# Four stacked-score attention phases: transposes three units back, the values of a sequence in one block, the first queries stacked from two queues

## The chip, the cores and the metric

The kernel runs on one core of a Trainium2 chip. The metric is the device time of one execution in microseconds (us). The kernel before takes 4164.63 us, the median of three runs (4161.31 to 4166.31).

## The reference

The reference sends x, 64 sequences of 128 tokens with 128 features, through eight layers, each added to x. Layers 1, 3, 5 and 7 are cross attention with 16 heads of 8 features to a context of 120 tokens for each sequence; layers 2, 4, 6 and 8 are feed-forward layers, three of them with a choice of experts, and the last one holds a causal self attention as well. In each attention:

```
scores = einsum('bhqd,bhkd->bhqk', Q, K) / sqrt(8)      # masks differ between the layers
attn   = softmax(scores, axis=-1)
out    = einsum('bhqk,bhkd->bhqd', attn, V)             # then @ Wo (+ bo), added to x
```

## The kernel before

x stays in SBUF for the whole program. The phases run one after the other: attention a0, feed-forward f0, a1, f1, a2, f2, a3, a second normalisation, the self attention s3, and f3. The change touches `attention_phase` where `packed` is true, and that is in a1, a2, a3 and s3. In profile rows the names of a1, a2 and a3 all read a_...; their stretches tell them apart: a1 lies at 560 to 1030 us, a2 at 1383 to 1876, a3 at 2482 to 2957, s3 (names s_...) at 2994 to 3503.

**Units.** A sequence has four units of four heads each, a group has four sequences and so 16 units, and a phase has 16 groups, 256 units. Each engine runs its own stream in order; semaphores join the streams. In slot s of a group the stream of TensorE (`group`, `behind`) holds: the scores of unit s (`scores`, line 792, and in a2, a3 and s3 a second matmul that adds the mask, line 798); the four transposes of unit s-2's probabilities (`turn`, line 807); in odd slots the values and the denominators of units s-5 and s-4 (`values`, line 831: 8 matmuls of 32 columns with the values vm, 8 with the ones dm); at s mod 4 = 2 the output projection of a sequence (`output`, lines 844 and 846); and at four slots a projection for the next group (`project`, one PSUM bank pj): keys at 0, turned x (ht) at 4, queries at 7 (a2: 8), values at 13; in s3 ht at 1, keys 4, queries 8, values 13.

VectorE takes unit s through a maximum (line 553) and a subtraction (line 558), with other work between the two: the reciprocal of a sequence's denominators at s mod 4 = 0 (line 566), the product with it at s mod 4 = 1 (line 572), normalisation of x for the next group (line 157) at slots 1 and 2, in s3 all four at slot 0, the sum with x at 7, statistics at 10, 11, 14, 15, and evictions of pj: queries in a2 (line 524, slot 8), values in a1 and a2 (line 541, slot 13). ScalarE does the exponentials (line 710), the evictions of the transposes into pt (`turned`, line 716) and the other evictions of pj. SC, the scores in PSUM, has two buffers: the scores of unit n wait for the subtraction of unit n-2. TP has two, PR (the probabilities) four, PT four.

**Stacking.** Keys and queries are split into a high and a low part, and three terms of each are stacked on 96 partitions: the high part is made by ScalarE (line 668), the low part by GpSimd (`low_part`, line 465), the stacking is 12 DMAs of keys and 12 of queries on the queue of SyncE (`stack_terms`, lines 404 and 410), and GpSimd spreads the keys over the heads (`masked_keys`, line 354). For the first group of a phase VectorE does units 1 and 3 of that, GpSimd 0 and 2, with the low part of the queries between them.

The lines that set the waits:

```
at_least(pe, sub_ready, n - 1)          # scores: unit n-2 subtracted
at_least(pe, pt_ready, n - 1)           # turn: unit n-2 out of TP
pe.wait_ge(pt_ready, n + 1)             # values: unit n in PT
dve.wait_ge(pv_done, b * U + U)         # reciprocals: all four units of b
```

## Time and profile before

| | us |
|---|---|
| median of three runs | 4164.63 |
| profiled execution, its own time | 4171.98 |
| its span | 4170.2 |
| TensorE busy in the span | 3419.6 (82%) |
| VectorE busy | 3345.5 (80%) |
| ScalarE busy | 2311.4 (55%) |
| GpSimd busy | 1568.3 (38%) |

The span is the profiled part of one execution, 1.8 us shorter than the execution's own time. Busy shares are means over phases that differ. The four phases of the change take about 1950 of the 4170 us. The granted TensorE clock is 1.00 (2.4 GHz) in the middle of each of them, and down to 0.50 (1.2 GHz) between phases and at their starts. In the timeline, the difference of the starts of two rows is how long the step really takes; the ends of matmuls are modelled.

### The profile page before, as it was taken

How to read it: one execution, taken by the hardware profiler on the slowest of the kernel's cores; microseconds unless marked ns; L12 is line 12 of the kernel's file. 1: busy time of each engine (PE TensorE's matmuls, PEld its weight loads, DVE VectorE, ACT ScalarE, POOL GpSimd, SP SyncE). 2: the span in 40 equal slices, each digit the busy share in tenths (PEclk: the TensorE clock that was granted, in tenths of full speed). 3: DMA queues.
4: the chain of work that ended last, by engine and by line, in shares of the span. 5: the costliest groups of instructions: out<-in, count | busy, mean ns of one | idle time of the engine just before them, and what ended most of it. 6: DMA issues, size and time to landing. Idle time of an engine off the chain costs nothing. (4 is left out here: it accounts for less than half of the span.)

```text
span 4170.2 us, 95372 instructions
## 1 busy us (share of the span) xinstructions
PE 3419.6 (82%) x31831; PEld 2495.1 (60%) x31831; DVE 3345.5 (80%) x6141; ACT 2311.4 (55%) x4244; POOL 1568.3 (38%) x911
## 2 busy tenths in 40 slices
PE   6983969998599799994038839999499998799999
PEld 3553646666477477774026626777366666677777
DVE  7888879998799799997025558999788888788888
ACT  2431647776277466661025526777577665466665
POOL 1210035553000355542754435555246553122222
PEclk9985979999599899995568969999799998899999
DMA  2001222221100222211111242222222222000000
GB/s 64 15 27 75 114 52 62 66 60 46 47 1 0 52 63 58 63 45 43 52 52 60 62 116 69 62 64 59 64 52 59 48 55 78 28 16 15 13 13 15
DMA packets 158967, 208.76 MB, mean 50 GB/s; under 512 B 37820, under 2 KB 109824, under 8 KB 155585
## 3 DMA queue, kind: packets, MB, share of 16 engines
q1 hardware_dynamic: 150593, 189.40, 16.7%
q0 software_dynamic: 8192, 16.92, 1.2%
q8 instruction: 115, 1.88, 0.2%
q14 instruction: 67, 0.55, 0.0%
HBM read 53.09 MB, written 42.21 MB: 23 GB/s over the span
## 5 line engine op out<-in xcount | busy, mean ns | idle before, releaser
L710 ACT ACTIVATE a_p<-a_p 128x480 f32<-128x480 f32 x832 | 501.6, 603 | 480.6 <-DVE a_p L558 477.9
L354 POOL TENSOR_TENSOR a_km<-a_k,a_slots 96x1920 fp32r<-96x1920 f32 x186 | 631.6, 3415 | 177.0 <-DMA a_k<-a_kh 177.0
L553 DVE TENSOR_REDUCE a_mx<-a_sc 128x4 f32<-128x480 f32 (+1 forms) x832 | 540.6, 650 | 98.3 <-PE a_sc L798 62.7
L558 DVE TENSOR_TENSOR a_p<-a_sc,a_mx 128x480 f32<-128x480 f32 x832 | 531.7, 639 | 18.8
L807 PE MATMUL a_tp<-ident,a_p 128*120 128x128 f32 x3328 | 518.5, 279 | 27.1 <-ACT a_p L710 25.9
L716 ACT ACTIVATE a_pt<-a_tp 120x512 f32<-120x512 f32 x832 | 485.9, 584 | 84.9 <-PE a_tp L807 84.1
L807 PEld LDWEIGHTS a_tp<-ident,a_p 128*120 128x120 f32 x3328 | 388.8, 139 | 136.7 <-ACT a_p L710 80.9
L792 PE MATMUL a_sc<-a_km,a_qr 96*128 96x480 f32 x768 | 395.7, 515 | 46.5 <-DMA a_qr<-a_ql 32.9
L831 PE MATMUL a_nd<-a_pt,a_vm 120*32 120x128 f32 x6656 | 274.9, 279 | 0.0
L1783 ACT ACTIVATE f_s<-f_pu 128x512 f32<-128x512 f32 x256 | 153.4, 599 | 212.8 <-PE f_pv L1265 212.8
L831 PE MATMUL a_nd<-a_pt,a_dm 120*32 120x128 f32 x6656 | 263.8, 273 | 0.0
L566 DVE RECIPROCAL a_rd<-a_nd 128x128 f32<-128x128 f32 x256 | 242.7, 948 | 8.0 <-PE a_nd L831 7.8
L354 POOL TENSOR_TENSOR s_km<-s_k,s_slots 96x2048 fp32r<-96x2048 f32 x62 | 223.9, 3630 | 55.2 <-DMA s_k<-s_kh 51.4
L1669 POOL TENSOR_TENSOR f_ya<-f_ya,f_yg 128x512 f32<-128x512 f32 x96 | 125.0, 1302 | 302.5 <-DVE f_yg L1719 302.4
L710 ACT ACTIVATE s_p<-s_p 128x512 f32<-128x512 f32 x256 | 161.1, 629 | 139.0 <-DVE s_p L558 139.0
L1694 DVE TENSOR_TENSOR f_a<-f_s,f_pv 128x512 f32<-128x512 f32 x256 | 175.4, 685 | 75.9 <-ACT f_s L1783 67.9
L792 PEld LDWEIGHTS a_sc<-a_km,a_qr 96*128 96x128 f32 x768 | 146.5, 191 | 141.1 <-issue 113.1
L1706 DVE TENSOR_TENSOR f_al<-f_a,f_ah 128x512 fp32r<-128x512 f32 x256 | 229.2, 895 | 0.0
L553 DVE TENSOR_REDUCE s_mx<-s_sc 128x4 f32<-128x512 f32 x256 | 175.2, 684 | 45.8 <-PE s_sc L798 45.6
L2094 PE MATMUL f_px<-ident,f_xr 128*128 128x128 f32 x128 | 24.6, 324 | 225.5 <-DMA f_xr<-dispatched 225.5
L831 PEld LDWEIGHTS a_nd<-a_pt,a_vm 120*32 120x32 f32 x6656 | 154.6, 109 | 76.6 <-ACT a_pt L716 39.3
L798 PE MATMUL a_sc<-a_addm,ident_bf 128*128 128x480 bf16 x512 | 195.8, 382 | 0.0
(429 smaller groups left out, 8843.3 us busy)
## 6 DMA issues: line engine op xcount, KB each, us to landing
a_qr<-a_qh SPq DMA_DIRECT2D x384, 64.0 KB, 2.0
a_k<-a_kh SPq DMA_DIRECT2D x384, 60.0 KB, 2.0
a_ctx<-in_ctxT SPq DMA_DIRECT2D x64, 240.0 KB, 2.7
a_qr<-a_ql SPq DMA_DIRECT2D x192, 64.0 KB, 2.0
a_k<-a_kl SPq DMA_DIRECT2D x192, 60.0 KB, 2.0
dispatched<-f_empty SPq DMA_DIRECT2D x8, 1040.0 KB, 21.0
f_xr<-dispatched SPq DMA_DIRECT2D x32, 260.0 KB, 2.6
chosen<-f_none SPq DMA_DIRECT2D x8, 1024.0 KB, 11.9
```

The source lines that it names most:

```text
L354: v.tensor_tensor(KM[par][:, i, :, :].rearrange("p b (j k) -> p b j k", k=KN), K3[:, i, :, :].unsqueeze(2).to_broadcast([TR, GB, 4, KN]), ...
L553: v.tensor_reduce(mx[:], view, AX.X, ALU.max).then_inc(mx_ready, 1)
L558: v.tensor_tensor(PR[s % 4][:].rearrange("p (h k) -> p h k", k=k), view, mx[:].unsqueeze(2).to_broadcast([P, heads, k]), ALU.subtract).the ...
L566: v.reciprocal(RD[:], ND[bt % 2][:, 1, :]).then_inc(rd_ready, 1)
L710: a.activation(PR[s % 4][:], PR[s % 4][:], ACT.Exp).then_inc(exp_ready, 1)
L716: a.activation(PT[s % 4][0:KN, :], TP[s % 2][0:KN, :], ACT.Copy).then_inc(pt_ready, 1)
L792: last = t.matmul(SC[s % 2][:, 0:W], queries, keys, start=True, stop=not masked)
L798: last = t.matmul(SC[s % 2][:, 0:W], R.ident_bf[:], addm[:].unsqueeze(1).to_broadcast([P, 4, KN]), start=False, stop=True)
L807: last = t.transpose(TP[s % 2][0:KN, q * P:(q + 1) * P], PR[s % 4][:, q * KN:(q + 1) * KN], R.ident[:])
L831: last = t.matmul(ND[j % 2][32 * q:32 * q + 32, what, :], w, PT[s % 4][0:KN, q * P:(q + 1) * P], start=(what == 0 and i == 0), stop=(i == ...
L1694: v.tensor_tensor(A[s % 2][:], S[s % 2][:], PV[s % 2][:], ALU.mult).then_inc(Z["a_ready"], 1)
L1706: v.tensor_tensor(AL[s % 4][:], A[s % 2][:], AH[s % 4][:].bitcast(F32), ALU.subtract).then_inc(Z["lo_ready"], 1)
```

## The change

It does four things, all where `packed` is true. TURN goes from 2 to 3, so that in slot s TensorE transposes unit s-3. The values and denominators of a sequence's four units stand together, in the slot where s mod 4 = 3 (32 matmuls), where before there were 16 in each of two odd slots. PT has eight buffers instead of four, with the wait in `turned` to match. And in the first group of a phase the low part of the queries is made by VectorE instead of GpSimd, and the query DMAs of units 0 and 1 go out on ScalarE's queue, those of 2 and 3 on SyncE's, without the waits on buffers (`stack_first`).

TensorE in a1, before, slots 6 and 7 of a group (pt2 is unit 2's buffer; sc, tp and nd are PSUM, km and qr stacked keys and queries; rows of line 48 and 839 set registers):

```order
L792 MATMUL a1_sc0<-a1_km0,a1_qr0 128x480
L807 MATMUL a1_tp0<-ident,a1_p0 120x128 x4
L839 REGISTER_ALU
L846 MATMUL a1_out<-a1_wo,a1_ct0 128x128
L48 REGISTER_ALU
L792 MATMUL a1_sc1<-a1_km0,a1_qr0 128x480
L807 MATMUL a1_tp1<-ident,a1_p1 120x128 x4
L831 MATMUL a1_nd1<-a1_pt2,a1_vm1 32x128 x4
L831 MATMUL a1_nd1<-a1_pt3,a1_vm1 32x128 x4
L831 MATMUL a1_nd1<-a1_pt2,a1_dm 32x128 x4
L831 MATMUL a1_nd1<-a1_pt3,a1_dm 32x128 x4
```

and now, slot 7 of the same group (slot 6 no longer has a block, nor has slot 5, where pt0 and pt1 stood before):

```order
L816 MATMUL a1_sc1<-a1_km0,a1_qr0 128x480
L831 MATMUL a1_tp0<-ident,a1_p0 120x128 x4
L48 REGISTER_ALU
L855 MATMUL a1_nd1<-a1_pt4,a1_vm1 32x128 x4
L855 MATMUL a1_nd1<-a1_pt5,a1_vm1 32x128 x4
L855 MATMUL a1_nd1<-a1_pt6,a1_vm1 32x128 x4
L855 MATMUL a1_nd1<-a1_pt7,a1_vm1 32x128 x4
L855 MATMUL a1_nd1<-a1_pt4,a1_dm 32x128 x4
L855 MATMUL a1_nd1<-a1_pt5,a1_dm 32x128 x4
L855 MATMUL a1_nd1<-a1_pt6,a1_dm 32x128 x4
L855 MATMUL a1_nd1<-a1_pt7,a1_dm 32x128 x4
```

All four units stand behind the scores and transposes of slot 7 and ahead of the next scores, and the transposes there turn p0 (unit 4) where they turned p1 (unit 5).

ScalarE at the start of a1, before (kh, qh are high parts, ql is the low part):

```order
L685 ACTIVATE a1_ht0<-a1_pj 128x512
L691 ACTIVATE a1_qt0<-a1_pj,a1_cols 128x512
L668 ACTIVATE a1_qh<-a1_qt0 128x512
L710 ACT_TABLE_LOAD
L710 ACTIVATE a1_p0<-a1_p0 128x480
```

and now:

```order
L703 ACTIVATE a1_ht0<-a1_pj 128x512
L709 ACTIVATE a1_qt0<-a1_pj,a1_cols 128x512
L686 ACTIVATE a1_qh<-a1_qt0 128x512
L764 DMA a1_qr0<-a1_qh 32x512 x2
L764 DMA a1_qr0<-a1_ql 32x512
L764 DMA a1_qr0<-a1_qh 32x512 x2
L764 DMA a1_qr0<-a1_ql 32x512
L728 ACT_TABLE_LOAD
L728 ACTIVATE a1_p0<-a1_p0 128x480
```

Six DMAs stand between the high part of the queries and the first exponential.

VectorE at the start of a1, before:

```order
L641 CAST a1_bo_terms<-a1_bo 1x128
L541 TENSOR_TENSOR a1_vm0<-a1_pj,a1_bv 120x16x4x8
L354 TENSOR_TENSOR a1_km0<-a1_k3,a1_slots 96x1920 x2
L553 TENSOR_REDUCE a1_mx0<-a1_sc0 128x4
L558 TENSOR_TENSOR a1_p0<-a1_sc0,a1_mx0 128x480
```

and now:

```order
L656 CAST a1_bo_terms<-a1_bo 1x128
L665 TENSOR_TENSOR a1_ql<-a1_qt0,a1_qh 128x512
L556 TENSOR_TENSOR a1_vm0<-a1_pj,a1_bv 120x16x4x8
L355 TENSOR_TENSOR a1_km0<-a1_k3,a1_slots 96x1920 x2
L568 TENSOR_REDUCE a1_mx0<-a1_sc0 128x4
L573 TENSOR_TENSOR a1_p0<-a1_sc0,a1_mx0 128x480
```

The low part of the queries has come in ahead of the first eviction of the values and of the two spreads of keys.

```diff
--- before.py
+++ after.py
@@ -251,7 +251,7 @@
     LN_SLOTS = (0, 0, 0, 0) if own_keys else (1, 1, 2, 2)
     SUM_SLOT, STATS_SLOTS = 7, (10, 11, 14, 15)
 
-    TURN, VALUES, RECIP, OUTPUT = (2, 4, 5, 7) if packed else (2, 3, 3, 4)
+    TURN, VALUES, RECIP, OUTPUT = (3, 4, 5, 7) if packed else (2, 3, 3, 4)
     KN = P if own_keys else KC
     U = 1 if hepos else 4
     S = GB * U
@@ -287,7 +287,8 @@
         VM = [sb(n_(f"vm{i}"), [P, GB, VW]) for i in range(2)]
         DM = sb(n_("dm"), [P, 4, 32])
         PR = [sb(n_(f"p{i}"), [P, W]) for i in range(4)]
-        PT = [sb(n_(f"pt{i}"), [P, 4 * P]) for i in range(4)]
+        TB = 8 if packed else 4
+        PT = [sb(n_(f"pt{i}"), [P, 4 * P]) for i in range(TB)]
         MX = [sb(n_(f"mx{i}"), [P, 16 if hepos else 4]) for i in range(2)]
         RD = sb(n_("rd"), [P, P])
         CT = [sb(n_(f"ct{i}"), [P, P]) for i in range(2)]
@@ -395,6 +396,19 @@
                 if hepos:
                     sp.dma_start(DM[0:KC, 0, :], I["classes"]).then_inc(weights_in, 16)
 
+                def stack_first():
+
+                    sp.wait_ge(low_ready["k"], 1)
+                    for i in range(4):
+                        for term, part in enumerate((HIGH, LOW, HIGH)):
+                            sp.dma_start(K3[32 * term:32 * term + 32, i, :, :].rearrange("p b k -> p (b k)"),
+                                         part["k"][32 * i:32 * i + 32, :].bitcast(F32)).then_inc(k3_in[i], 16)
+                    sp.wait_ge(low_ready["q"], 1)
+                    for i in (2, 3):
+                        for term, part in enumerate((HIGH, HIGH, LOW)):
+                            sp.dma_start(QR[0][32 * term:32 * term + 32, i, :].bitcast(F32),
+                                         part["q"][32 * i:32 * i + 32, :].bitcast(F32)).then_inc(q3_in[i], 16)
+
                 def stack_terms(g, par):
 
                     sp.wait_ge(low_ready["k"], g + 1)
@@ -416,7 +430,7 @@
                     for i in range(3):
                         sp.dma_start(bo3[i:i + 1, :], bo_terms[:, i, :]).then_inc(bo3_in, 16)
                 if own_keys:
-                    groups_loop(sp, lambda g, par, first, last: stack_terms(g, par), 3)
+                    groups_loop(sp, lambda g, par, first, last: stack_first() if first else stack_terms(g, par), 3)
                     return
                 ctx_load(1, 1)
                 if hepos:
@@ -426,7 +440,7 @@
 
                     pairs_loop(sp, NG - 2, pair)
                     return
-                stack_terms(0, 0)
+                stack_first()
 
                 def pair(g):
                     ctx_load(g + 2, 0)
@@ -465,17 +479,18 @@
                     nc.gpsimd.tensor_tensor(LOW[step][:], src, HIGH[step][:].bitcast(F32),
                                             ALU.subtract).then_inc(low_ready[step], 1)
 
-                def prepare(g, par, others=(1, 2, 3)):
+                def prepare(g, par):
                     low_part("k", g)
                     masked_keys(pool, nc.gpsimd, g, par, (0,))
                     low_part("q", g)
-                    masked_keys(pool, nc.gpsimd, g, par, others)
+                    masked_keys(pool, nc.gpsimd, g, par, (1, 2, 3))
 
                 def group(g, par, first, last):
                     if not last:
                         prepare(g + 1, 1 - par)
 
-                prepare(0, 0, (2,))
+                low_part("k", 0)
+                masked_keys(pool, nc.gpsimd, 0, 0, (0, 2))
                 groups_loop(pool, group)
 
             @block.vector
@@ -645,6 +660,9 @@
                             dve.wait_ge(bo_split, 2 * i + 2)
                 if mask is not None:
                     q_evict(0, 0)
+                if packed:
+                    dve.wait_ge(high_ready["q"], 1)
+                    v.tensor_tensor(LOW["q"][:], QT[0][:], HIGH["q"][:].bitcast(F32), ALU.subtract).then_inc(low_ready["q"], 1)
                 if bv is not None:
                     v_evict(0, 0, True)
                 if packed:
@@ -712,8 +730,8 @@
                 def turned(g, s):
                     n = g * S + s
                     act.wait_ge(tp_ready, n + 1)
-                    at_least(act, pv_done, n - 3)
-                    a.activation(PT[s % 4][0:KN, :], TP[s % 2][0:KN, :], ACT.Copy).then_inc(pt_ready, 1)
+                    at_least(act, pv_done, n - TB + 1)
+                    a.activation(PT[s % TB][0:KN, :], TP[s % 2][0:KN, :], ACT.Copy).then_inc(pt_ready, 1)
 
                 def group(g, par, first, last):
                     for s in range(S):
@@ -739,6 +757,12 @@
                     evict(step, 0, 0)
                     if packed and step in "kq":
                         high_part(step, 0)
+                    if packed and step == "v":
+                        act.wait_ge(low_ready["q"], 1)
+                        for i in (0, 1):
+                            for term, part in enumerate((HIGH, HIGH, LOW)):
+                                act.dma_start(QR[0][32 * term:32 * term + 32, i, :].bitcast(F32),
+                                              part["q"][32 * i:32 * i + 32, :].bitcast(F32)).then_inc(q3_in[i], 16)
                 groups_loop(act, group, 3 if U == 1 else 1)
 
             @block.tensor
@@ -829,7 +853,7 @@
                                 w = VM[par][0:KN, j, 32 * h:32 * h + 32]
 
                             last = t.matmul(ND[j % 2][32 * q:32 * q + 32, what, :], w,
-                                            PT[s % 4][0:KN, q * P:(q + 1) * P],
+                                            PT[s % TB][0:KN, q * P:(q + 1) * P],
                                             start=(what == 0 and i == 0), stop=(i == U - 1), skip_group_check=True,
                                             tile_position=(0, 32 * q))
                     if 1 in whats:
@@ -853,10 +877,9 @@
                     if U == 1:
                         if not (first and s < VALUES) and s - VALUES < S:
                             values(g, s - VALUES, par if s >= VALUES else 1 - par)
-                    elif s % 2 == 1 and not (first and s < VALUES) and s - VALUES < S:
-                        two = (s - VALUES - 1, s - VALUES)
+                    elif s % U == U - 1 and not (first and s < VALUES) and s - VALUES < S:
                         for what in range(2):
-                            for u in two:
+                            for u in range(s - VALUES - U + 1, s - VALUES + 1):
                                 values(g, u, par if s >= VALUES else 1 - par, (what,))
                     u = s - OUTPUT
                     if not (first and u < 0) and (u + 1) % U == 0:
```

## Rows read from the trace of the kernel before

**Rows 1.** a3: length, busy us of PE, PEld, DVE, ACT, POOL; clock; DMA.

```profile
2560.00:2880.00 320.00, 317.75 (x4251) 230.93 (x4248) 292.71 (x558) 233.90 (x433) 179.78 (x69) 1.00 0.25 63
```

**Rows 2.** Stretches of a1, a2, a3, s3: line 553 alone, one reduction for each unit.

```profile
640.00:960.00 320.00, 117.96 (x182) 1.00 0.26 63
...
1440.00:1760.00 320.00, 114.97 (x177) 1.00 0.25 62
...
2560.00:2880.00 320.00, 118.01 (x182) 1.00 0.25 63
...
3040.00:3360.00 320.00, 115.67 (x169) 1.00 0.23 55
```

**Rows 3.** Timeline of a3's last group: start us, us long, engine, line, out<-in.

```profile
2933.96 0.65 DVE L558 TENSOR_TENSOR a_p<-a_sc,a_mx 128x480 f32<-128x480 f32 x1
...
2935.30 0.65 PE L807 MATMUL a_tp<-ident,a_p 128*120 128x128 f32 x4
...
2935.88 0.64 PE L831 MATMUL a_nd<-a_pt,a_vm 120*32 120x128 f32 x16
...
2936.34 0.62 PE L831 MATMUL a_nd<-a_pt,a_dm 120*32 120x128 f32 x16
...
2936.89 0.48 PE L792 MATMUL a_sc<-a_km,a_qr 96*128 96x480 f32 x1
...
2937.43 0.60 PE L807 MATMUL a_tp<-ident,a_p 128*120 128x128 f32 x4
...
2937.63 0.66 DVE L553 TENSOR_REDUCE a_mx<-a_sc 128x4 f32<-128x480 f32 x1 [0.37 <-PE a_sc L798]
...
2939.07 0.59 DVE L558 TENSOR_TENSOR a_p<-a_sc,a_mx 128x480 f32<-128x480 f32 x1
...
2940.34 0.65 DVE L558 TENSOR_TENSOR a_p<-a_sc,a_mx 128x480 f32<-128x480 f32 x1
```

**Rows 4.** Waits of the weight loads in the same stretch of a3.

```profile
PEld a_sc L792 <- issue: 16.5, 80, 0.2
...
PEld a_nd L831 <- issue: 7.9, 46, 0.2
```

**Rows 5.** Timeline, a1: a score matmul that waits for a score buffer.

```profile
804.29 0.65 DVE L558 TENSOR_TENSOR a_p<-a_sc,a_mx 128x480 f32<-128x480 f32 x1
...
804.99 0.48 PE L792 MATMUL a_sc<-a_km,a_qr 96*128 96x480 f32 x1 [0.47 <-DVE a_p L558]
```

**Rows 6.** Timeline, a1's last group: scores, and the reduction of the same unit.

```profile
1010.67 0.48 PE L792 MATMUL a_sc<-a_km,a_qr 96*128 96x480 f32 x1
...
1011.20 0.66 DVE L553 TENSOR_REDUCE a_mx<-a_sc 128x4 f32<-128x480 f32 x1 [0.15 <-PE a_sc L792]
```

**Rows 7.** Timeline, a3: a query projection right behind a block of values.

```profile
2718.93 1.12 PE L760 MATMUL a_pj<-a_ht,a_wq 128*128 128x512 f32 x2
...
2720.53 0.66 DVE L553 TENSOR_REDUCE a_mx<-a_sc 128x4 f32<-128x480 f32 x1 [0.92 <-PE a_sc L798]
```

**Rows 8.** Timeline, a1: VectorE work between a reduction and its subtraction.

```profile
803.68 0.69 DVE L541 TENSOR_TENSOR a_vm<-a_pj,a_bv 120x512 f32<-120x512 f32 x1 [0.51 <-PE a_pj L769]
...
810.46 0.59 DVE L157 TENSOR_SCALAR a_h<-x,a_mean,a_rstd 128x128 f32 x2
```

**Rows 9.** Timeline, s3: normalisation of a group, and two reciprocals in its last group.

```profile
3203.75 1.59 DVE L157 TENSOR_SCALAR s_h<-x,s_mean,s_rstd 128x128 f32 x4
...
3483.89 0.95 DVE L566 RECIPROCAL s_rd<-s_nd 128x128 f32<-128x128 f32 x1
...
3490.47 0.95 DVE L566 RECIPROCAL s_rd<-s_nd 128x128 f32<-128x128 f32 x1
```

**Rows 10.** Timeline, the start of a1.

```profile
572.89 3.17 POOL L465 TENSOR_TENSOR a_ql<-a_qt,a_qh 128x512 fp32r<-128x512 f32 x1
...
575.25 2.83 DVE L354 TENSOR_TENSOR a_km<-a_k,a_slots 96x1920 fp32r<-96x1920 f32 x1 [0.30 <-DMA a_k<-a_kh]
...
587.67 0.66 DVE L553 TENSOR_REDUCE a_mx<-a_sc 128x4 f32<-128x480 f32 x1 [1.96 <-PE a_sc L792]
```

## The prediction

> **What bounds the kernel now.** I first asked, stretch by stretch, which engine is full. In a3 TensorE is busy 317.75 of 320 us at full clock, VectorE 292.71 [rows 1]. Then I counted reductions, one for each unit, to get the time of a group: 320/182 x 16 = 28.1 us in a1, 320/177 x 16 = 28.9 in a2, 28.1 in a3 and 320/169 x 16 = 30.3 in s3 [rows 2]. TensorE and VectorE are both nearly full in each, so neither sum tells what a longer block in one slot does. For that I followed one lap: the chain from a subtraction to the subtraction four units later, through both engines. It can be read off the last group of a3, where no projections stand between.
>
> From the subtraction of unit 5 (2933.96) to its transposes in slot 7 are 1.34 us (the exponential lies in them), to the values 0.58, to the denominators 0.46, to the scores of unit 8 0.55, to their reduction 0.74, through the reciprocal to the subtraction of unit 8 1.44, and to that of unit 9 1.27 [rows 3]. The sum is 6.38 us for a sequence, and VectorE's wait of 0.37 ahead of unit 8's reduction says that TensorE's block was what it waited for. So light sequences go at the pace of this lap; in the other groups projections on TensorE are added, and in a2 and a3 fill it.
>
> **The block of four units.** The scores of unit n need the subtraction of n-2, since there are two score buffers. With the values of four units in slot 7, the lap goes: subtraction of unit 5, scores of unit 7, transposes of unit 4, 32 matmuls, scores of unit 8, its reduction, reciprocal and subtraction, unit 9. Step by step:
> - subtraction to the scores two units on: 0.70 [rows 5];
> - scores to transposes: 0.54 (2936.89 to 2937.43); transposes to values: 0.58 [rows 3];
> - the block: 0.46 + 0.55 = 1.01 for two units as now. The other two add 2 x 0.46 = 0.92 at most. At the least they add 1.01 less the 16.5/80 = 0.20 us in which the weight loads stand still after a block [rows 4], 0.81. I take 0.87;
> - 0.74, 1.44 and 1.27 as before [rows 3].
>
> The sum is 7.15 us (7.09 to 7.20) where the lap now is 6.38. TURN = 3 takes the exponential out of the lap, but that gives back only 0.10: subtraction to values was 1.34 + 0.58 = 1.92 and is 0.70 + 0.54 + 0.58 = 1.82, since the wait for a score buffer comes to stand where the wait for the exponential was. What waits behind the block is the next scores, and VectorE behind these: at the block's start it has at most two units in hand.
>
> Without the mask matmul (a1) scores to reduction is 0.53 [rows 6] instead of 0.74; I take the same 0.21 off scores to transposes, and get 7.15 - 0.42 = 6.73. In s3 the light lap now is 3490.47 - 3483.89 = 6.58, 0.20 above a3's [rows 9], so 7.35.
>
> **What else lies on the lap.** Work on VectorE between unit 8's reduction and unit 9's subtraction, and on TensorE between slot 7 and the scores of slot 8, adds to it; the rest is now hidden in the light slots, where TensorE only waits. On the lap are: half of a group's normalisation, at slot 1 (0.59 for two, of which some 0.5 shows [rows 8]); in a1 and a2 the eviction of the values at slot 13, 804.29 - 803.68 = 0.6 [rows 5, 8]; in a2 the eviction of the queries, of the same size, at slot 8, 0.6; in a1 and a3 the query projection behind the block of slot 7: 2720.53 - 2718.93 = 1.60 to the reduction against 0.74 without it, so 0.86 [rows 7]; in s3 all four normalisations at slot 0, some 1.5 [rows 9]. Keys, ht and values are projected in slots 0, 1, 4 and 13, off the lap.
>
> A group then takes: a1 4 x 6.73 + 0.5 + 0.86 + 0.6 = 28.9 (now 28.1, +0.8); a2 28.6 + 0.5 + 0.6 + 0.6 = 30.3 (28.9, +1.4); a3 28.6 + 0.5 + 0.86 = 30.0 (28.1, +1.9); s3 29.4 + 1.5 = 30.9 (30.3, +0.6). Together +4.7, and over 15 groups +70. The 16th has no projections and loses the bare difference of the laps: 4 x 0.77 = 3.1 in a2, a3 and s3, and 4 x 0.56 = 2.2 in a1 (its lap now lacks 0.21 once, the new one twice), +11.5.
>
> **The first queries.** Now GpSimd makes the low part in 3.17 us between two spreads of keys, and all 12 query DMAs follow it; the fourth unit is reduced at 587.67, after 1.96 us of waiting [rows 10]. In the new order the low part is on VectorE as soon as the high part is there, half of the DMAs go out beside the others, and the scores are ready when VectorE ends its second spread (575.25 + 2.83 = 578.1 [rows 10]). From there four reductions and three subtractions with two pairs of normalisation between them are 4.9 us, so the fourth unit comes at 583.0, 4.6 us earlier. The six DMA issues on ScalarE's queue lie ahead of its first exponential, which has some 9 us to spare. Bounds: nothing, if the low part on VectorE has to wait for GpSimd's spread of keys, which runs beside it, up to 4.6, four times. s3 does four normalisations in its first slot, so I take 16 us in all (0 to 18). At the end of a phase the last block is longer by one pair's denominators and starts: 0.46 each, +2.
>
> The sharing of a port bears on this term alone. GpSimd's low part took 3.17 us beside VectorE's spreads [rows 10]. The Trainium skill, SBUF — State Buffer, Who interferes with whom, says that a VectorE instruction with two inputs in SBUF contends with a GpSimd instruction that reads SBUF; this row agrees, and by the rule the moved low part may in its turn stand behind a spread, which would take up to 3 us off the 4.6 in a phase.
>
> **The buffers.** Eight PT buffers cost no time; they let four units be held until slot 7. The last of them, unit 3, is evicted by ScalarE before the values need it: it is the fourth of the block.
>
> **Sum.** 70 + 11.5 - 16 + 2 = +68. Against the profiled execution's own 4172 us that is 4240; the runs' median is 4164.6, and I predict 4233.
>
> **Rivals.**
> *TensorE's sum decides, and the kernel gets faster.* For it: TensorE is full in a3 [rows 1], and the weight loads stand still 7.9/46 = 0.17 us before a block and 0.20 after [rows 4]. One block less for each sequence takes that away once: two blocks of values cost 2 x (0.17 + 1.01) = 2.36, one of four 0.17 + 1.01 + 0.92 = 2.10, so 0.26 x 64 x 4 = 67 us. With the starts: 4165 - 67 - 16 + 2 = 4084. Against it: this needs VectorE to be fed through a slot of 0.54 + 0.58 + 1.88 + 0.74 = 3.7 us from scores to next reduction, with two units of 1.3 us in hand. It decides if the lap is below 28.1/4 less 0.26, 6.8.
> The Trainium skill, TensorEngine Tiling (Array Packing), Key Properties, says that a change of the tiling mode drains TensorE. Rows 4 agree with it, and by that rule alone this rival would be right.
> *A draw.* The lap comes to 6.9, for instance because the block goes at the weight loads' pace and the waits for score buffers are shorter than in rows 5. Then 0.25 x 256 = 64 us go from my sum and it ends at 4169, within 0.2% (8 us, about what a measurement of this kernel can tell from no change).
> *Slower still.* In a1 the lap with its extras gives 4 x 6.17 + 1.96 = 26.6 for a group that takes 28.1. If the new groups run above their lap by 1 us as well, 60 us come on top: 4293.
>
> **How the numbers follow.** Forecast 0.75, own range 4195 to 4280: the second pair at its bounds is 0.06 x 256 = 15 us either way, the starts 16 less or 2 more, and some of the third rival's excess. Faster rival 0.12, draw 0.07, slower still 0.06. The range 4190 to 4280 leaves out the faster rival and part of the draw and of the last. Faster by over 0.2% 0.12, same 0.07, slower 0.81.
>
> **What would show it.** Reciprocals of light sequences 7.1 to 7.2 us apart in a2 and a3, 6.7 in a1. VectorE's wait for scores: one of about 1 us in each sequence, on the reduction at s mod 4 = 0, and hardly any other; in a3 far above the present sum. TensorE's wait for the exponential gone, and in its place one for the subtraction, ahead of the scores of slot 7. TensorE's busy time in a3 some 0.9 of the stretch. First units 2 to 5 us earlier in each phase. I am wrong if the reciprocals of the light sequences are under 6.9 us apart, or if TensorE is still full in a3.

## The result: slower by 2.3%

| kernel | median of the runs, us | ratio to the kernel before |
|---|---|---|
| before | 4162.97 | 1 |
| changed | 4261.1 (4258.99 to 4267.75) | 1.0235 [1.0222, 1.0249] |

Both medians are of four runs. The change costs 98 us. The forecast was 4233, own range 4195 to 4280, slower with a chance of 0.81. The span of the profiled execution is 4265.9 us, 95.7 more than before.

The first thing to read again is a3, the stretch of [rows 1]:

```profile
core 0: us, PE busy (x) PEld busy (x) DVE busy (x) ACT busy (x) POOL busy (x), PEclk, DMA share, GB/s
2560.00:2880.00 320.00, 301.39 (x4001) 222.06 (x4003) 274.72 (x521) 220.42 (x405) 171.46 (x65) 1.00 0.24 59
```

TensorE was busy 317.75 us of 320 and now is 301.39, at the same clock; VectorE went from 292.71 to 274.72. Both are busy for a smaller share, so the time went into waits between them. The page's costliest groups say which (busy us, mean ns of one, then idle time ahead and its releaser). In the kernel before:

```profile
L553 DVE TENSOR_REDUCE a_mx<-a_sc 128x4 f32<-128x480 f32 (+1 forms) x832 | 540.6, 650 | 98.3 <-PE a_sc L798 62.7
...
L807 PE MATMUL a_tp<-ident,a_p 128*120 128x128 f32 x3328 | 518.5, 279 | 27.1 <-ACT a_p L710 25.9
...
L792 PE MATMUL a_sc<-a_km,a_qr 96*128 96x480 f32 x768 | 395.7, 515 | 46.5 <-DMA a_qr<-a_ql 32.9
```

and in the changed one:

```profile
L568 DVE TENSOR_REDUCE a_mx<-a_sc 128x4 f32<-128x480 f32 (+1 forms) x832 | 540.9, 650 | 167.6 <-PE a_sc L822 115.9
...
L816 PE MATMUL a_sc<-a_km,a_qr 96*128 96x480 f32 x768 | 398.9, 519 | 143.0 <-DVE a_p L573 125.5
...
L831 PE MATMUL a_tp<-ident,a_p 128*120 128x128 f32 x3328 | 506.9, 275 | 6.1 <-ACT a_pt L734 5.1
```

VectorE is idle 167.6 us ahead of its reductions, where it was 98.3. TensorE waits 125.5 us for subtractions ahead of its scores, where before it waited mostly for DMAs (32.9 of 46.5). The transposes' wait for the exponential is gone. Each engine waits for the other once in a lap, the round from one reciprocal to the next through both. One lap of a3's last group, which answers to [rows 3]:

```profile
3001.15 0.66 DVE L568 TENSOR_REDUCE a_mx<-a_sc 128x4 f32<-128x480 f32 x1 [1.16 <-PE a_sc L822]
...
3001.72 0.95 DVE L581 RECIPROCAL a_rd<-a_nd 128x128 f32<-128x128 f32 x1
...
3002.59 0.59 DVE L573 TENSOR_TENSOR a_p<-a_sc,a_mx 128x480 f32<-128x480 f32 x1
...
3003.24 0.48 PE L816 MATMUL a_sc<-a_km,a_qr 96*128 96x480 f32 x1 [0.81 <-DVE a_p L573]
...
3003.78 0.60 PE L831 MATMUL a_tp<-ident,a_p 128*120 128x128 f32 x4
3003.86 0.65 DVE L573 TENSOR_TENSOR a_p<-a_sc,a_mx 128x480 f32<-128x480 f32 x1
3004.21 0.39 PE L870 MATMUL a_out<-a_wo,a_ct 128*128 128x128 f32 x2
...
3004.56 0.48 PE L816 MATMUL a_sc<-a_km,a_qr 96*128 96x480 f32 x1
...
3005.10 0.60 PE L831 MATMUL a_tp<-ident,a_p 128*120 128x128 f32 x4
...
3005.63 1.08 PE L855 MATMUL a_nd<-a_pt,a_vm 120*32 120x128 f32 x32
...
3006.53 1.06 PE L855 MATMUL a_nd<-a_pt,a_dm 120*32 120x128 f32 x32
...
3007.51 0.48 PE L816 MATMUL a_sc<-a_km,a_qr 96*128 96x480 f32 x1
...
3008.25 0.66 DVE L568 TENSOR_REDUCE a_mx<-a_sc 128x4 f32<-128x480 f32 x1 [0.69 <-PE a_sc L822]
...
3008.82 0.95 DVE L581 RECIPROCAL a_rd<-a_nd 128x128 f32<-128x128 f32 x1
```

From reciprocal to reciprocal are 3008.82 - 3001.72 = 7.10 us. The steps, start to start: reciprocal to subtraction 0.87, to the scores two units on 0.65, to the transposes 0.54, to the output projection 0.43, to the next scores 0.35, to the transposes 0.54, to the values 0.53, through the block 3007.51 - 3005.63 = 1.88, from the scores to their reduction 0.74, to the reciprocal 0.57. That is the forecast's lap of 7.15. One detail differs: TensorE's wait (0.81) stands one unit earlier than I put it, ahead of the scores with s mod 4 = 2. The way from that subtraction over the next one (1.27 + 0.70) is exactly as long as the one over TensorE's queue (0.65 + 0.54 + 0.43 + 0.35 = 1.97), so both stand on the lap.

The table has the times between reciprocals, read off the timeline, by the slot from which and to which they run. In the middle groups of a phase they hold steady to 0.02 from group to group, but where means are named. "Light" is a sequence without projections, evictions or normalisations.

| phase | kernel | 0 to 4 | 4 to 8 | 8 to 12 | 12 to 0 | group |
|---|---|---|---|---|---|---|
| a1 | before | 7.49 | 7.16 | 6.17 | 7.37 | 28.2 |
| a1 | after | 7.66 | 7.61 | 6.67 | 7.27 | 29.2 |
| a2 | before | 7.49 | 6.53 | 7.20 | 7.68 | 28.9 |
| a2 | after | 7.88 | 7.10 | 7.73 | 7.71 | 30.4 |
| a3 | before | 7.40 | 7.39 | 6.38 | 7.02 | 28.2 |
| a3 | after | 7.79 | 7.96 | 7.10 | 7.1 to 7.2 | 30.0 |
| s3 | before | 8.37 (mean) | 7.55 | 7.33 | 7.15 | 30.4 |
| s3 | after | 9.17 (mean; 8.36 to 10.7) | 7.97 | 7.76 | 7.30 | 32.2 |

### The profile page after: what moved, and what is told of

Read it like the earlier page. It is cut to its first block and busy times, and to the rows that moved or that the text cites. A ratio compares the mean times of both kernels' runs of the same rounds, so it can differ in the third digit from the quotient of the medians.

```text
span 4265.9 us, 95453 instructions
## 1 busy us (share of the span) xinstructions
PE 3416.3 (80%) x31830; PEld 2529.6 (59%) x31831; DVE 3347.9 (78%) x6145; ACT 2319.8 (54%) x4244; POOL 1553.2 (36%) x907
## 3 DMA queue, kind: packets, MB, share of 16 engines
q8 instruction: 115, 1.88, 0.2%
q10 hardware_dynamic: 1152, 1.57, 0.2%
## 5 line engine op out<-in xcount | busy, mean ns | idle before, releaser
L568 DVE TENSOR_REDUCE a_mx<-a_sc 128x4 f32<-128x480 f32 (+1 forms) x832 | 540.9, 650 | 167.6 <-PE a_sc L822 115.9
L573 DVE TENSOR_TENSOR a_p<-a_sc,a_mx 128x480 f32<-128x480 f32 x832 | 532.3, 640 | 19.1 <-issue 0.3
L816 PE MATMUL a_sc<-a_km,a_qr 96*128 96x480 f32 x768 | 398.9, 519 | 143.0 <-DVE a_p L573 125.5
L831 PE MATMUL a_tp<-ident,a_p 128*120 128x128 f32 x3328 | 506.9, 275 | 6.1 <-ACT a_pt L734 5.1
L831 PEld LDWEIGHTS a_tp<-ident,a_p 128*120 128x120 f32 x3328 | 403.5, 138 | 85.6 <-issue 35.2
L855 PE MATMUL a_nd<-a_pt,a_vm 120*32 120x128 f32 x6656 | 234.8, 276 | 0.0
L855 PE MATMUL a_nd<-a_pt,a_dm 120*32 120x128 f32 x6656 | 228.6, 273 | 0.0
L855 PEld LDWEIGHTS a_nd<-a_pt,a_vm 120*32 120x32 f32 x6656 | 166.1, 109 | 43.5 <-issue 36.8
```

The source lines that it names most:

```text
L568: v.tensor_reduce(mx[:], view, AX.X, ALU.max).then_inc(mx_ready, 1)
L573: v.tensor_tensor(PR[s % 4][:].rearrange("p (h k) -> p h k", k=k), view, mx[:].unsqueeze(2).to_broadcast([P, heads, k]), ALU.subtract).the ...
L816: last = t.matmul(SC[s % 2][:, 0:W], queries, keys, start=True, stop=not masked)
L831: last = t.transpose(TP[s % 2][0:KN, q * P:(q + 1) * P], PR[s % 4][:, q * KN:(q + 1) * KN], R.ident[:])
L855: last = t.matmul(ND[j % 2][32 * q:32 * q + 32, what, :], w, PT[s % TB][0:KN, q * P:(q + 1) * P], start=(what == 0 and i == 0), stop=(i == ...
```

## Experiments

All ratios are to the kernel before, timed on the same chip, with a 95% interval.

**The block of four units, taken out again.**

```diff
-                    elif s % U == U - 1 and not (first and s < VALUES) and s - VALUES < S:
+                    elif s % 2 == 1 and not (first and s < VALUES) and s - VALUES < S:
...
-                            for u in range(s - VALUES - U + 1, s - VALUES + 1):
+                            for u in (s - VALUES - 1, s - VALUES):
```

> The changed kernel with values and denominators of two units together again; turning three units back, eight buffers and the early first queries stay. Theory A (the block of four units lengthens the lap of each sequence): the lap goes from 7.15 to 6.28 us, 0.10 under that of the kernel before, and the time to 4135 to 4165 us, since the first queries stay early. Theory B (turning three units back, or the waits on more buffers, cost as much as the block does): it stays above 4200. Theory C (the merged blocks save drains on TensorE, and the loss is elsewhere): no faster than 4240.

Measured: 4148.48 us, 0.9957 [0.9943, 0.9971], faster than before. The light laps are 6.35 in a3 and 6.25 in a1. It is a small difference, but the interval leaves out 1. Without the block the rest of the change gains 16 us; the block on top of it costs 4261 - 4148 = 113. Theories B and C fall.

**The block alone, turning two units back.** The kernel before with the two lines above the other way round, and eight buffers.

> The kernel before with the values and denominators of four units together and eight buffers, and nothing else: turning two units back, first queries as they were. Theory A (the block alone): the exponential stands in the lap, 1.34 + 0.58 + 1.01 + 0.87 + 0.74 + 1.44 + 1.27 = 7.25 us, so light sequences of a3 have their reciprocals 7.2 to 7.3 apart, and the time is 4265 to 4295 us. Theory B (turning three units back is what costs): under 4215. Were the four units' longer turn hidden, the exponential would not show, and the laps would be 7.1 as in the changed kernel.

Measured: 4329.53 us, 1.0388 [1.0371, 1.0405]. The light laps are 7.25 in a3 and 7.04 in a1, the latter again 0.21 less, as worked out. The total is 35 us above my range: the sequences with projections, which the sum took to differ by the same 0.10, take 8.21 and 8.26 in a3 where the changed kernel has 7.79 and 7.96. There ScalarE has an eviction and a high part to do as well, and with TURN = 2 the exponential behind them is on the lap. In one such sequence (its transposes at 2716.86) they wait 0.38 us for it. TURN = 3 and the early first queries together so give back 68 us of what the block costs without them; the next experiment puts the queries' part at 5.

**The early first queries alone.** `TURN = 2`, pairs, four buffers, and the new order of the first low parts and DMAs.

> The kernel before with the early first queries alone. Theory A (as predicted): the fourth unit of a1, a2 and a3 comes 4 to 5 us earlier, s3's less, and the time is 4149 us (4145 to 4155). Theory B (what the trace of the changed kernel shows at s3's start, where VectorE's second spread runs beside GpSimd's and is 2.3 us longer, holds everywhere): the gain is under 5 us in all, 4158 to 4168.

Measured: 4159.9 us, 0.9987 [0.9977, 0.9996]: 5 us, not 16. Theory B. From the high part of the queries to the reduction of the fourth unit it takes 18.1, 18.5, 17.0 and 19.4 us in a1, a2, a3 and s3, where the kernel before takes 20.3, 20.2, 19.1 and 19.8: 2.2, 1.8, 2.1 and 0.4 less, 6.4 in all. The start of a1 in the changed kernel shows the mechanism; it answers to [rows 10]:

```profile
569.77 3.45 DVE L355 TENSOR_TENSOR a_km<-a_k,a_slots 96x1920 fp32r<-96x1920 f32 x1 [1.30 <-DMA a_k<-a_kh]
...
571.63 4.83 POOL L355 TENSOR_TENSOR a_km<-a_k,a_slots 96x1920 fp32r<-96x1920 f32 x1 [0.42 <-DMA a_k<-a_kh]
...
573.49 4.99 DVE L355 TENSOR_TENSOR a_km<-a_k,a_slots 96x1920 fp32r<-96x1920 f32 x1 [0.27 <-DMA a_k<-a_kh]
578.40 0.64 DVE L568 TENSOR_REDUCE a_mx<-a_sc 128x4 f32<-128x480 f32 x1
...
583.75 0.64 DVE L568 TENSOR_REDUCE a_mx<-a_sc 128x4 f32<-128x480 f32 x1
```

VectorE's second spread took 2.83 us and takes 4.99. In these rows the two engines do not slow each other down, they wait for each other in the order in which they start. GpSimd's spread (571.63) starts while VectorE's first one runs until 573.22, and so takes 4.83 us where 3.38 is its usual time; VectorE's second (573.49) starts while that one runs until 571.63 + 4.83 = 576.46, and ends at 578.48, 2.02 later. In all fourteen kept traces, a spread of VectorE that starts beside a running instruction of GpSimd (a spread or a low part) ends 2.01 to 2.02 us after that one's end, and in s3 2.14 to 2.15, 100 cases in all. The only one that meets none, the second of a3 in twelve of the traces, takes 2.14. By the same count the old 2.83 was a wait of 0.82 until the low part's end (572.89 + 3.17 = 576.06) and 2.02 behind it. The fourth unit comes at 583.75, not 583.0, and of its 3.9 us the phase's earlier start is 1.7.

In a3 the moved low part itself waits, as the prediction feared: it starts 0.17 us behind GpSimd's first spread and takes 3.75 us, where it takes 0.69 in the other three phases.

```profile
2532.94 3.38 POOL L355 TENSOR_TENSOR a_km<-a_k,a_slots 96x1920 fp32r<-96x1920 f32 x1 [3.25 <-DMA a_k<-a_kh]
2533.11 3.75 DVE L665 TENSOR_TENSOR a_ql<-a_qt,a_qh 128x512 fp32r<-128x512 f32 x1 [5.63 <-ACT a_qh L686]
```

**The reciprocal off the lap.** In the changed kernel:

```diff
-    SUM_SLOT, STATS_SLOTS = 7, (10, 11, 14, 15)
+    SUM_SLOT, STATS_SLOTS = (11, (12, 13, 14, 15)) if packed else (7, (10, 11, 14, 15))
-    TURN, VALUES, RECIP, OUTPUT = (3, 4, 5, 7) if packed else (2, 3, 3, 4)
+    TURN, VALUES, RECIP, OUTPUT = (3, 4, 7, 10) if packed else (2, 3, 3, 4)
```

> The changed kernel with the reciprocals two slots later (from s mod 4 = 0, right behind VectorE's wait for the block, to s mod 4 = 2), the normalised product one unit after them at s mod 4 = 3, the output projection at s mod 4 = 1, ahead of scores that wait for a subtraction, and the sum of the residual at slot 11 with its statistics at 12 to 15. Theory A (one lap through both engines sets the pace): the reciprocal leaves the lap, reduction to subtraction goes from 1.44 to 0.75 us, the light lap of a3 from 7.10 to about 6.4, and since TensorE is then nearly full again, a group of a3 comes to 27.5 to 28.5 us: 4110 to 4170 us in all. Theory B (VectorE's or TensorE's total decides, or the block's length by itself): moving the reciprocal changes neither total, light laps stay at 7.0 or more, and the time stays above 4230.

Four things move here: the reciprocals, their products, the output projection, and the sum with its statistics. Measured: 4177.42 us, 1.0023 [1.001, 1.0037]. The same instructions in the same numbers, and 84 of the 98 us are back, 7 above the top of theory A's range. Theory B falls. In a3's last group:

```profile
2928.35 0.95 DVE L581 RECIPROCAL a_rd<-a_nd 128x128 f32<-128x128 f32 x1
...
2928.99 1.08 PE L855 MATMUL a_nd<-a_pt,a_vm 120*32 120x128 f32 x32
...
2930.88 0.48 PE L816 MATMUL a_sc<-a_km,a_qr 96*128 96x480 f32 x1
...
2931.61 0.66 DVE L568 TENSOR_REDUCE a_mx<-a_sc 128x4 f32<-128x480 f32 x1 [0.48 <-PE a_sc L822]
...
2932.38 0.66 DVE L573 TENSOR_TENSOR a_p<-a_sc,a_mx 128x480 f32<-128x480 f32 x1
...
2934.42 0.48 PE L816 MATMUL a_sc<-a_km,a_qr 96*128 96x480 f32 x1 [0.19 <-DVE a_p L573]
...
2934.84 0.95 DVE L581 RECIPROCAL a_rd<-a_nd 128x128 f32<-128x128 f32 x1
```

Behind the block the reduction is followed by its subtraction in 0.77 us instead of 1.44, and the lap is 6.49. That is the reciprocal's part (0.67), and the light laps lost nearly as much (7.10 - 6.49 = 0.61); how the 84 us divide between the four moves was not tried. The reciprocal (2928.35) now ends 0.3 us into TensorE's block (2928.99 to 2930.88), and no matmul waits for it there.

**The query projection out of slot 7** (a1 and a3, `7` to `8` in the table of slots).

> The changed kernel with the query projection of a1 and a3 one slot later, in slot 8 instead of behind the block in slot 7. Theory A (in slot 7 it lies on the lap, 0.86 us a group): the sequence from slot 4 to slot 8 of a3 goes from 7.97 to 7.1 us, that of a1 from 7.61 to 6.7. The next one may get up to 0.45 longer by ScalarE's evictions, as in s3 (7.76 against 7.30 without). So a group gains 0.4 to 0.86, over 15 groups of two phases 12 to 26 us: 4235 to 4250. Theory B (TensorE's total sets the time of a group): the projection costs the same in either slot, 4257 to 4266.

Measured: 4251.55 us, 1.0221 [1.0192, 1.025]; the interval overlaps the changed kernel's, and the time lies between the ranges of the two theories. The sequence from slot 4 to 8 fell by exactly 0.86, in a3 from 7.96 to 7.10 and in a1 from 7.61 to 6.75, so it was on the lap with all its length. But the next one rose, to 7.62 in a3 and to 7.50 (by 0.83) in a1. The group gains 0.35 in a3 and nothing in a1.

**Pairs, with the late reciprocals.**

> The kernel with the reciprocals two slots later, and with values and denominators of two units together instead of four. It says what the merged block is worth where the lap leaves it room. Theory A (merging saves TensorE next to nothing, the lap is all there is to it): light sequences of a3 under 6.35 us, the time 4120 to 4155. Theory B (a block less saves TensorE the 0.26 us of a sequence that the rival had): slower than the merged one with late reciprocals, above 4177, and a group of a3 at 28.2 us or more, against 27.74.

Measured: 4221.86 us, 1.0149 [1.012, 1.0178], where the same step won 84 us with the block of four. Not theory A. It is what B said in numbers (a3's group 29.3), but most of it is not B's reason, as the next one shows.

**The same with the output projection one slot on** (`OUTPUT = 11`).

> The kernel with pairs and late reciprocals (4222 us, where I had expected 4120 to 4155) with the output projection one slot later: at s mod 4 = 2 instead of s mod 4 = 1, where the other pair of values stands. Theory A (the output projection, 0.43 us, lies in one slot with a pair, and the reciprocal right behind that pair: two pieces on the lap that the kernel before has apart): it falls by 0.43 for most sequences, 60 to 110 us: 4115 to 4165. Theory B (the reciprocal behind the second pair is the whole of it, wherever the projection stands): no less than 4205.

Measured: 4179.64 us, 1.0046 [1.0032, 1.006]: 42 us back, between the two theories. With pairs there is a block in the slots with s mod 4 = 1 too. The moved projection (0.43) stood in one slot with it, and the moved reciprocal stands right behind it still. So the place of a piece of work is good or bad only against the blocks; the rest, 31 us, I put down to the reciprocal, but did not try that by itself.

**s3's normalisations, two attempts and a base with pairs.** The changed kernel's excess in s3 is in the sequence that has them. In one of its long cases:

```profile
3147.68 3.60 POOL L355 TENSOR_TENSOR s_km<-s_k,s_slots 96x2048 fp32r<-96x2048 f32 x1
...
3150.57 1.57 DVE L157 TENSOR_SCALAR s_h<-x,s_mean,s_rstd 128x128 f32 x4
...
3152.29 0.63 PE L781 MATMUL s_pj<-ident,s_h 128*128 128x128 f32 x4 [1.89 <-DVE s_h L157]
...
3154.63 0.77 PE L816 MATMUL s_sc<-s_km,s_qr 96*128 96x512 f32 x1 [0.18 <-DVE s_p L573]
...
3155.64 1.06 PE L831 MATMUL s_tp<-ident,s_p 128*128 128x128 f32 x4
...
3156.63 1.39 PE L855 MATMUL s_nd<-s_pt,s_vm 128*32 128x128 f32 x32
...
3159.58 0.69 DVE L568 TENSOR_REDUCE s_mx<-s_sc 128x4 f32<-128x512 f32 x1 [2.21 <-PE s_sc L822]
```

```profile
core 0: us, PE busy (x) PEld busy (x) DVE busy (x) ACT busy (x) POOL busy (x), PEclk, DMA share, GB/s
...
3149.00:3153.00 4.00, 2.11 (x16) 1.50 (x14) 3.90 (x8) 0.82 (x2) 2.29 (x1) 1.00 0.12 28
3153.00:3158.00 5.00, 4.82 (x54) 3.45 (x58) 3.90 (x7) 4.38 (x8) 0.00 (x0) 0.66 0.00 2
```

The normalisations take 1.57 us where they meet GpSimd's spread, which ends at 3151.28 (1.09 in the next group, where they don't meet it). TensorE is busy only 2.11 of 4 us, and in the next stretch its clock is granted at 0.66 on average, between the levels 2.4 and 1.2 GHz: transposes of 0.60 take 1.06. This sequence took 10.49 us; 5 of 14 were above 10, the others 8.36 to 8.73. In all five the clock was granted at 0.66 to 0.71 over the 5 us behind the wait, and that wait of TensorE for the normalisations was 1.80 to 2.34 us; in the nine others it was 1.33 to 1.65. First attempt:

```diff
-    LN_SLOTS = (0, 0, 0, 0) if own_keys else (1, 1, 2, 2)
+    LN_SLOTS = (1, 1, 2, 2)
-    ... else (1, 4, 8, 13)))
+    ... else (4, 6, 8, 13)))
```

> The changed kernel with s3's four normalisations in slots 1, 1, 2 and 2 as in the other phases, instead of all in slot 0; its transposes of h move from slot 1 to 4 and its key projection from 4 to 6. Theory A (s3 lost 16 us more than predicted, since the four normalisations leave TensorE idle up to 1.9 us, it then runs at the lower clock for some 3 us, and in some groups they meet GpSimd's spread): the sequence from slot 0 to 4 goes from 9.17 us (mean; 8.35 to 10.7) to about 7.9, steadily, and the time falls by 15 to 22 us: 4239 to 4246. Theory B (s3's excess comes from ScalarE's evictions at the key and query projections): that sequence falls by the half of the normalisations that leaves the lap, 0.7 us, but the others get as much longer: 4250 to 4265.

Measured: 4268.71 us, 1.0262 [1.0233, 1.0291], no gain, and above the ranges of both theories. The sequence still takes 8.62 to 11.6. The later key projection brought GpSimd's last spread into slot 1, and the two normalisations there took 1.35 us, in the bad cases with the clock's fall behind them. With pairs as the base:

> Turning three units back, eight buffers and early first queries with blocks of two units (4148 us), and s3's normalisations, transposes and key projection moved as in the run before. Theory A: its sequence from slot 0 to 4 (mean 9.17 us; in the kernel before 8.37) falls to about 7.5, so 15 x 1.6 = 24 us less: 4120 to 4132. Theory B (with blocks of two units TensorE's total decides in s3, and the work only moves): 4140 to 4150.

Measured: 4172.26 us, 1.0029 [1.001, 1.0048], 24 slower than its base and again above both ranges. Its trace has the worst meeting (GpSimd's three spreads end at 3145.62):

```profile
3134.91 10.71 POOL L355 TENSOR_TENSOR s_km<-s_k,s_slots 96x2048 fp32r<-96x2048 f32 x3
...
3143.35 2.61 DVE L157 TENSOR_SCALAR s_h<-x,s_mean,s_rstd 128x128 f32 x2
3147.08 0.59 DVE L157 TENSOR_SCALAR s_h<-x,s_mean,s_rstd 128x128 f32 x2
```

Two normalisations take 0.59 without GpSimd. The first pair takes 2.61, because it waits for the end of the third spread and is done 0.34 us later, at 3145.96. Second attempt, `(2, 2, 3, 3)` for s3:

> The changed kernel with s3's normalisations in slots 2, 2, 3 and 3, its transposes of h in slot 4 and its key projection in slot 6. In slot 1 two of them took 1.35 us beside GpSimd's spread, TensorE waited 1.3 for the subtraction behind them, and in some groups its clock then fell to the lower level for 5 us. Theory A (that stall is what s3 lost beyond the sum): in slot 3 VectorE waits for the block anyway, so the sequence from slot 0 to 4 comes to 7.3 to 8.0 us in every group, against a mean of 9.17, and the time to 4238 to 4248. Theory B (the later key projection shifts GpSimd's spreads into other slots, and they cost there what they cost here): 4255 to 4275.

Measured: 4239.16 us, 1.0175 [1.0158, 1.0192]: 22 less. The sequence takes 7.61 to 7.67 in 12 of 14 groups, 8.01 and 8.07 in the other two. Theory A. The granted clock of 3100 to 3480 went from 0.98 to 1.00.

> Turning three units back, eight buffers and early first queries with blocks of two units (4148 us), with s3's normalisations, transposes and key projection placed as in the run before. Theory A: 15 x 1.3 us = 20 less, 4122 to 4135, the fastest so far. Theory B: 4145 to 4175.

Measured: 4150.56 us, 0.9963 [0.9949, 0.9977], the same as its base. Theory B: seven of 14 groups take 30.0 to 30.1 but the others 31.5 to 32.3 us, and the scores wait 15.1 us for GpSimd's spreads, which the later key projection delays.

**Both pieces off the lap, with the block of four.** `RECIP = 7, OUTPUT = 10` and `(2, 2, 3, 3)` for s3.

> The block of four units with both pieces of work off its lap: reciprocals two slots later in all phases (4177 us alone), and s3's normalisations in slots 2, 2, 3 and 3 with its transposes of h in slot 4 and its key projection in slot 6 (22 us less alone). Theory A (the two add up, since they lie in different places of the lap): s3's sequence with the normalisations falls from 9.3 us (mean) to 7.2 to 7.8 and the time to 4145 to 4160, not slower than the kernel before (4165). Theory B (with both in slots 1 to 3 VectorE's work in slot 2, a reciprocal and two normalisations, delays the scores of slot 4): 4165 to 4185.

Measured: 4181.3 us, 1.004 [1.0026, 1.0055]. The time lies in theory B's range: the two gains don't add up. But the waits of s3 (3080 to 3500) name another reason than theory B's:

```profile
POOL s_kl L479 <- ACT s_kh L686: 146.0, 13, 12.4
...
PE s_sc L816 <- POOL s_km L355: 23.9, 16, 2.4
```

TensorE waits for the spread keys 16 times. GpSimd itself is idle 146 us: it is not full, its input comes too late. Eight of this kernel's 14 s3 groups take 30.83 to 30.85 us, the others 31.5 to 33.8. In the second attempt 12 of 14 take 30.82 to 30.86, and there TensorE waits for the spread keys once in a group, up to 0.6 us. I read that as the chain from key projection to spread keys (slot 6 to slot 3 of the next group) being the new bound. This is not shown: a kernel with the key projection earlier wasn't run.

None of these beats the pairs with TURN = 3 and early queries: 4148 us, 0.43% under the kernel before.

## Why the prediction was right, and where its sizes were off

From the first to the last reciprocal of a phase, the growth against the forecast (15 groups and the last one's 3.1 or 2.2):

| phase | forecast | measured |
|---|---|---|
| a1 | 12.0 + 2.2 = 14.2 | 452.91 - 436.01 = 16.9 |
| a2 | 21.0 + 3.1 = 24.1 | 472.73 - 448.01 = 24.7 |
| a3 | 28.5 + 3.1 = 31.6 | 466.04 - 436.49 = 29.6 |
| s3 | 9.0 + 3.1 = 12.1 | 497.81 - 469.33 = 28.5 |
| starts and the rest | -16 + 2 = -14 | 95.7 - 99.7 = -4 |

The forecast was 28 us too low. Of that 16 are in s3, 10 at the starts and 3 in a1; a3 was put 2 too high.

- *The lap.* Right, in sign and size: 7.10 for 7.15, 6.67 for 6.73 (a1), 7.30 for 7.35 (s3). The block's second pair is 1.88 - 1.01 = 0.87. Two experiments show that it is the lap: without the block the growth is gone, and with the reciprocal and what hangs on it moved 84 us come back while no engine has less to do.
- *TURN = 3 gives back only 0.10.* Nearly right for light sequences of a3 (7.25 against 7.10, 0.15), too little for those with evictions on ScalarE (0.3 to 0.4), and for a1 (7.04 against 6.67). The forecast didn't need it, as it went straight to the new lap.
- *What else lies on the lap.* The query projection's 0.86 was exact. The normalisations, put at 0.5 a group, cost 0.69 in a3, 0.78 in a2 and 0.99 in a1, by the sequence from 0 to 4 less the light one; why a1's is the largest stays open. The mis-sized term is s3. I put its keys "off the lap" and left its queries out; measured against the light 7.30 they cost 0.67 and 0.46 a group, 15 x 1.13 = 17 us. TensorE itself has room there, but ScalarE's eviction and high part delay the turned copies: the transposes wait for them 20 times in 3180 to 3500, up to 0.5 us. The normalisations were put at 1.5 and cost 8.42 - 7.30 = 1.1 in an undisturbed group, but in five groups TensorE's clock fell, some 1.9 us each. The 1.5 itself was read off a row ([rows 9]) that stands beside a spread of GpSimd.
- *The first queries.* Predicted 16, alone 5. The step that failed is "the scores are ready when VectorE ends its second spread (575.25 + 2.83)": that 2.83 held a wait for the rest of GpSimd's low part only. With the low part gone, GpSimd's next spread starts earlier and VectorE's second one waits for it: 12.75 us from the high part of the queries to the first reduction, not 10.7. That the first reduction came at 578.40 in absolute time, near the 578.1 forecast, is luck: the phase had started 1.7 earlier. The Trainium skill, SBUF — State Buffer, Who interferes with whom, says that a VectorE instruction with two inputs in SBUF contends with a GpSimd instruction that reads SBUF; the traces agree (4.99 for 2.83). I had applied it to the moved low part alone. There it held in a3 (3.75 us for 0.69); in the other three phases the low part was over before GpSimd's first spread, and what cost the time were the two spreads.
- *TensorE's sum decides* (the faster rival) fell on its condition: the lap is not below 6.8. What it would be worth can be bounded, but no run shows it. In a3 a group takes 27.86 with pairs and TensorE full, and 27.74 with the block of four and late reciprocals and TensorE busy 314.49 of 320:

```profile
2560.00:2880.00 320.00, 319.94 (x4323) 231.78 (x4323) 295.92 (x565) 235.62 (x436) 181.93 (x69) 1.00 0.25 63
```

```profile
2560.00:2880.00 320.00, 314.49 (x4331) 237.18 (x4329) 292.40 (x565) 237.54 (x440) 180.86 (x70) 1.00 0.26 63
```

  The first row is the pairs', the second the other's. Busy time is no price for a block: the same instructions come to 27.26 us a group here (314.49/320 x 27.74) and to 28.3 in the changed kernel (301.39/320 x 30.03). By the starts of rows, one block of four takes 1.88 where two pairs take 2.02, and one wait of the weight loads ahead of a block (0.17, [rows 4]) falls away: 0.14 to 0.31 us a sequence, an estimate that holds the forecast's 0.26. The Trainium skill (TensorEngine Tiling (Array Packing), Key Properties) says that a change of the tiling mode drains TensorE. The standstills around a block agree, but they are worth at most 0.31 us a sequence by this estimate, where the longer block adds 0.87 to the lap.
- *What would show it.* VectorE waits ahead of the reduction at s mod 4 = 0, 1.16 and 0.69 us in the rows; TensorE is busy 0.94 of a3, where I said some 0.9; the exponential's wait is gone, and the subtraction's is one unit earlier than I said. The fourth units came 2.2, 1.9, 2.1 and 0.8 us earlier in a1, a2, a3 and s3, counted from the high part of the queries, where I had said 2 to 5 in each.

## What to carry to other kernels

Where two engines feed each other through two buffers, as here, the longest piece of work on one engine between two hand-overs can set the pace, even if both engines then become idler; follow one lap through both before merging work to save starts. If a block must be long, keep the other engine's first step behind it short: moving the reciprocal, and the work that hangs on it, by two slots was worth 84 us. A duration read beside one neighbour is no duration beside another: for each instruction moved off an engine, ask what that engine does in its place.

## What the runs showed of the hardware that I had not expected

- Between VectorE and GpSimd the one that starts later waited, in these instructions, for the whole rest of the other's. A spread of VectorE ends 2.01 to 2.02 us (s3: 2.14 to 2.15) after the GpSimd instruction that ran at its start, whether that makes it 2.64 us long (a3 before) or 5.35 (a3 after). A normalisation that waits ends 0.08 to 0.09 us after it, in all 56 cases of the changed kernel. In a3 a start 0.04 us behind GpSimd's (2536.79 against 2536.75) made a spread 5.35 us long.
- TensorE's clock fell inside a phase that is 0.9 busy: after 1.89 us of waiting and a thin stretch (2.11 busy of 4 us) it ran at the lower level for some 3 us. Normalisations that took 1.48 to 2.03 us, where nine other groups had 1.02 to 1.34, so made the sequence 1.9 us longer. A wait of 1.40 us in the next group did not bring it down, and neither did one of 1.85 us in the kernel before (granted clock 1.00 from 3388 to 3393).
- The block of four units (32 matmuls of the program, 64 in the profile's rows) takes 1.88 us, 29 ns a row; its second half adds 0.87, 27 ns a row.
